# Output projection of a small transformer layer transposed and issued between attention steps, on one core

## The chip, the cores and the metric

The kernel runs on one core of a Trainium2 chip. The metric is the device time of one execution in microseconds (us); smaller is better. All times below are microseconds unless marked ns.

## The reference

`x` is 32 sequences of 112 tokens with 512 features. Two layers follow each other; the first is a cross-attention over a context of 375 tokens. The second, which the change touches, takes the 14 best tokens of each sequence by a router score, 448 in all, and runs a transformer block on them:

```
h = rms_norm(sel) ; q, k, v = h@wq+bq, h@wk+bk, h@wv+bv        # 16 query heads, 8 key heads of 128
att = softmax(causal(q_rot @ k_rot.T / sqrt(128)))             # 448 x 448 per head
x1  = sel + (att @ v).reshape(448, 2048) @ wo                  # output projection
mlp = (silu(rms_norm(x1) @ w_gate) * (rms_norm(x1) @ w_up)) @ w_down
out = sigmoid(score) * (x1 + mlp) + (1 - sigmoid(score)) * x   # scattered back to the tokens
```

## The kernel before, in words

The first layer is a software pipeline over 32 sequences and fills most of the span; the change leaves it alone. The second layer works on S = 448 tokens as NC = 4 tiles of L = 112, features as KC = 4 tiles of P = 128. Each engine has its instructions written out in order in its own function, and semaphores tie the engines together. An engine that waits holds up everything behind it on that engine.

Precision: `mm3` (L1211) multiplies two float32 matrices as three products of rounded parts (hi x hi, hi x lo, lo x hi, type fp32r). ScalarE makes the rounded part, GpSimd or VectorE the rest. Attention itself and the output projection use plain float32 matmuls, which the profile shows as two instructions each.

Attention runs over k = 0 to 63, head k // 4, query tile c = k % 4, with (c + 1) x 112 keys. For step k TensorE's `att` (L1471) makes the scores in PSUM bank c and adds the mask (L1472). VectorE takes the negated row maximum (L1146). ScalarE takes the exponential with the row sum (L847), VectorE divides by the sum (L1137, L1140). LAG = 3 steps later TensorE transposes the probabilities (`turn_probs`, L1480) into bank 4 or 5 in turn, and ScalarE empties that bank (`turn_evac`, L837). Once a head's four tiles are there, `weigh` (L1490) multiplies by the values into bank 6 or 7 in turn, and VectorE copies the result to `attnT` (L1152). ScalarE's order in one step is the exponential of k, then emptying of k - 3.

After the last head TensorE makes the projection (L1506) in 128 instructions, with tokens on partitions, one PSUM bank per token tile. VectorE adds the residual (L1170), sums squares (L1173); ScalarE takes the root (L799); VectorE scales (L1097); TensorE transposes 16 tiles (L1439), and the rounded part and the rest (L806, L1111) go to `hT_hi`, `hT_lo`. Meanwhile VectorE computes the sigmoid gates (L1156 to L1167).

The feed-forward loop runs over j = 0 to 15 blocks of 128 hidden features: gate and up products (24 matmuls of 448 columns), SiLU on ScalarE (L879) and VectorE (L1191 to L1197), rounding of the hidden block (L862) and its rest (L1184), and two blocks later `down`, 12 matmuls of 512 columns with tokens on partitions. GpSimd makes the rests of the weights (L620, L629). At the end VectorE adds (L1205) and gates (L1207) each token tile and GpSimd scatters it (L633).

SyncE's queue loads `wo` before attention, w_gate and w_up when attention begins and w_down (4 MB, L455) after the projection, because `w_down` lies where `wo` lay.

## Time and profile before

| | |
|---|---|
| median of 3 runs | 1685.36 us (1683.93 to 1686.45) |
| profiled execution: time / span of its instructions | 1689.02 / 1687.3 us |
| TensorE busy, whole span | 1602.7 us, 95% |
| VectorE / ScalarE / GpSimd busy | 65% / 41% / 40% |
| mean granted TensorE clock | 0.977 |

Rows of the timeline give start (us from the span's start), length, engine, line, operation, output<-inputs, shape and count, and in brackets the idle time before with what ended it. PE is TensorE, DVE VectorE, ACT ScalarE, POOL GpSimd, PEld TensorE's weight loads. Matmuls overlap: the distance between starts, not the length, is what each adds in a full stream. Rows of a stretch give its bounds and length, then busy time and count of PE, PEld, DVE, ACT and POOL, the granted TensorE clock (1.00 is 2.4 GHz, 0.50 is 1.2 GHz), the DMA share and GB/s. Rows of a group end with busy us, mean ns | idle time before.

### The profile page before, as it was taken

Reading aid. Unit: us, or ns where it says so; the run is one execution under the profiler, and the core shown is the slowest. Engines: PE = TensorE matmul, PEld = TensorE weight load, DVE = VectorE, ACT = ScalarE, POOL = GpSimd, SP = SyncE. Lnnn points to the kernel's source line nnn. Section 1 sums busy time; section 2 is a strip of 40 time slices with the busy share of each in tenths; the row PEclk is TensorE's granted clock in tenths of the full one; section 3 lists DMA queues with packets and bytes.
Section 4 is the critical chain, followed back from the end, with each engine's and each line's share of the span. In section 5 each row is a group of like instructions: output and inputs, shape, how many; then the busy total and the mean of one; then the engine's idle time right before and its main releaser. Section 6 shows DMA issues by size and latency. Waiting matters only on the chain.

```text
span 1687.3 us, 43831 instructions
## 1 busy us (share of the span) xinstructions
PE 1602.7 (95%) x17669; PEld 1224.4 (73%) x17669; DVE 1096.7 (65%) x1751; ACT 686.4 (41%) x1406; POOL 678.3 (40%) x758
## 2 busy tenths in 40 slices
PE   7999999999999999999999999999974999898997
PEld 5776777777777777777777777777763876645885
DVE  5754667766767667776677767776663856622766
ACT  5763444344443444434444444434432225511331
POOL 6762443443434443444434434344323950011542
PEclk9999999999999999999999999999985999998999
DMA  6841111221112211121111211122056013002000
GB/s 186 246 123 62 48 53 45 63 68 45 51 45 65 66 45 51 45 74 56 51 45 48 77 51 51 45 63 67 28 190 212 1 40 161 1 0 100 1 1 22
DMA packets 66103, 113.71 MB, mean 67 GB/s; under 512 B 21328, under 2 KB 36016, under 8 KB 64512
## 3 DMA queue, kind: packets, MB, share of 16 engines
q1 hardware_dynamic: 65216, 110.20, 20.6%
q0 software_dynamic: 832, 2.75, 0.6%
q8 instruction: 37, 0.61, 0.2%
q14 instruction: 18, 0.15, 0.0%
HBM read 82.59 MB, written 30.34 MB: 67 GB/s over the span
## 4 chain that ended last, share of the span: by engine, by line
PE 91%; DVE 3%; ACT 2%; issue 1%; DMA 1%; POOL 1%; SPq 0%; ACTq 0%; DVEq 0%; POOLq 0%
PE ps L1213 20%; PE ps L1214 17%; PE ps L1215 17%; PE ps L1340 11%; PE ps L1315 7%; PE ps L1506 3%; PE ps L1265 3%; PE ps L1288 3%; PE ps L1490 2%; PE ps L1318 1%; PE ps L1471 1%; PE ps L1480 1%; PE ps L1247 1%; PE ps L1295 1%; PE ps L1228 0%
## 5 line engine op out<-in xcount | busy, mean ns | idle before, releaser
L939 DVE RECIPROCAL rec<-ps 128x224 f32<-128x224 f32 x128 | 199.2, 1556 | 98.6 <-PE ps L1340 95.6
L499 POOL TENSOR_TENSOR prob_img<-prob 128x448 f32<-128x448 f32 x128 | 157.4, 1230 | 235.9 <-PE ps L1340 214.7
L462 POOL TENSOR_TENSOR ctx_lo<-ctx_raw,ctx_hi 128x472 fp32r<-128x472 f32 x64 | 115.3, 1826 | 288.7 <-ACT ctx_hi L644 288.7
L701 ACT ACTIVATE prob<-ps 119x448 f32<-119x448 f32 x128 | 69.7, 545 | 249.3 <-PE ps L1318 249.3
L934 DVE TENSOR_REDUCE top<-ps 112x4 f32<-112x1028 f32 x128 | 156.2, 1221 | 0.0
L1315 PEld LDWEIGHTS ps<-q_all,k_all 32*128 32x128 f32 (+1 forms) x3072 | 121.6, 186 | 40.1 <-issue 31.8
L1315 PE MATMUL ps<-q_all,k_all 32*128 32x112 f32 (+1 forms) x3072 | 148.0, 300 | 1.4 <-ACT prob L703 1.4
L933 DVE TENSOR_REDUCE top<-ps 112x4 f32<-112x472 f32 x128 | 83.0, 648 | 84.7 <-PE ps L1288 84.7
L677 ACT ACTIVATE sq_junk<-proj 128x513 bf16<-128x513 f32 (+1 forms) x96 | 61.1, 637 | 184.4 <-DVE proj L913 184.4
L703 ACT ACTIVATE prob<-ps 128x896 f32<-128x896 f32 x128 | 117.0, 914 | 0.0
L620 POOL TENSOR_TENSOR ring_lo<-ring,gate_up_hi 128x512 fp32r<-128x512 f32 x32 | 42.1, 1338 | 169.8 <-ACT gate_up_hi L855 169.8
L1213 PE MATMUL ps<-w_v_img_hi,ctx_hi 128*128 128x512 f32 x256 | 107.3, 419 | 0.5
L1213 PE MATMUL ps<-w_k_img_hi,ctx_hi 128*128 128x512 f32 x256 | 107.4, 420 | 0.0
L1215 PE MATMUL ps<-w_v_img_hi,ctx_lo 128*128 128x512 f32 x256 | 101.1, 395 | 0.0
L1215 PE MATMUL ps<-w_k_img_hi,ctx_lo 128*128 128x512 f32 x256 | 101.1, 395 | 0.0
L1214 PE MATMUL ps<-w_k_img_lo,ctx_hi 128*128 128x512 f32 x256 | 100.9, 394 | 0.0
L1214 PE MATMUL ps<-w_v_img_lo,ctx_hi 128*128 128x512 f32 x256 | 100.9, 394 | 0.0
L1215 PE MATMUL ps<-hT_hi,ring_lo 128*128 128x448 f32 x224 | 83.6, 373 | 0.0
L1318 PE MATMUL ps<-topT,pick_img 32*128 32x112 f32 x1024 | 80.8, 296 | 0.0
L493 POOL TENSOR_TENSOR rstd<-sq_sum,neg_half 128x1 f32<-128x1 f32 x96 | 52.8, 549 | 56.1 <-ACT sq_junk L677 56.1
L967 DVE SCALAR_TENSOR_TENSOR equal<-ps,score_now,later 112x112 f32<-112x112 f32 x32 | 10.7, 335 | 92.7 <-PE ps L1300 92.7
L1213 PEld LDWEIGHTS ps<-w_v_img_hi,ctx_hi 128*128 128x128 f32 x256 | 47.9, 187 | 21.7 <-DVE proj L913 7.7
(297 smaller groups left out, 4372.5 us busy)
## 6 DMA issues: line engine op xcount, KB each, us to landing
ctx_raw<-in_ctx_dram SPq DMA_DIRECT2D x32, 748.0 KB, 4.2
xh_dram<-xh SPq DMA_DIRECT2D x32, 448.0 KB, 3.1
q_dram<-q_turned SPq DMA_DIRECT2D x28, 256.0 KB, 2.8
q_all<-q_dram SPq DMA_DIRECT2D x32, 224.0 KB, 3.1
xh<-in_x_dram SPq DMA_DIRECT2D x32, 224.0 KB, 2.8
out_dram<-out_sb SPq DMA_DIRECT2D x32, 224.0 KB, 2.3
xa<-in_x_dram SPq DMA_DIRECT2D x21, 256.0 KB, 3.4
ring<-in_wq_dram SPq DMA_DIRECT2D x1, 4096.0 KB, 13.8
```

The source lines that it names most:

```text
L462: nc.gpsimd.tensor_tensor(ctx_lo[:, :, cols], ctx_raw[:, :, cols], ctx_hi[:, :, cols].bitcast(F32), ALU.subtract).then_inc(ctx_lo_done, 1)
L499: nc.gpsimd.tensor_tensor(prob_img[:], prob[:, g % 2, 1, :], prob[:, g % 2, 2, :], ALU.add).then_inc(img_summed, 1)
L703: nc.scalar.activation(prob[:, g % 2, 1:3, :].rearrange("p c (j q) -> p j c q", j=GH), ps[:, 2:6, L:3 * L].rearrange("p j (c q) -> p j c q ...
L933: nc.vector.tensor_reduce(rows[:, :, 2 * g], ps[0:L, 2:6, 0:TXT], AX.X, ALU.max)
L934: nc.vector.tensor_reduce(rows[:, :, 2 * g + 1], ps[0:L, 2:6, TAIL:CTX], AX.X, ALU.max).then_inc(s_done, 1)
L939: nc.vector.reciprocal(rec[:], bank[:, 2:4]).then_inc(norm_step, 1)
L1213: nc.tensor.matmul(o_, a_hi, b_hi, start=start, stop=False)
L1214: nc.tensor.matmul(o_, a_hi, b_lo, start=False, stop=False)
L1215: return nc.tensor.matmul(o_, a_lo, b_hi, start=False, stop=stop)
L1315: nc.tensor.matmul(ps[0:rows, 2 + j, out_cols], k_all[head, g, cols], q_all[head, g, :], start=True, stop=False)
L1318: last = nc.tensor.matmul(ps[0:rows, 2 + j, out_cols], pick[head, g, :], topT[g // 2][head, :], start=False, stop=True)
L1340: last = nc.tensor.matmul(ps[HD * j:HD * (j + 1), bank, slot * L:(slot + 1) * L], left[0:rows, cols], right[0:rows, L * j:L * (j + 1)], st ...
```

## The change

The projection is turned round: its output and everything after it up to the end of the feed-forward loop has features on partitions and 448 token columns. It uses `mm3` on rounded attention output (`attn_hi`, `attn_lo`) and rounded weights (`wo_hi` by ScalarE, `wo_lo` by GpSimd), and is issued one head at a time inside the attention loop (`output_T`). Its sum stays in PSUM banks 0 to 3 through the loop, so attention has two score banks (4, 5), one for transposes (6) and one for weighing (7). The residual enters that sum as 16 float32 matmuls with the identity (head 0). Sums of squares over partitions are matmuls with a column of ones; the root is transposed back to a row. `down` multiplies into the same four banks, whose contents ScalarE has copied to `mid_raw`; at the end 16 transposes turn the result back. ScalarE empties the transposed tile of step k - 3 before it takes the exponential of step k. The gate computations move to the value products before attention and into its first steps; w_down is loaded in four pieces as the heads of `wo` are used up. The diff, cut (moved gate code, buffers and semaphores left out; 12 leading blanks removed):

```diff
-sp.wait_ge(mid_full, NC)
-sp.dma_start(w_down, t["w_down"].rearrange("(c p) n -> p c n", p=P)).then_inc(ring_loaded[2], 16)
+for e in range(4):
+    sp.wait_ge(ring_loaded[2], 16 * e + 16)
+    if e < 3:
+        sp.wait_ge(o_step, 4 * e + 4)
+    else:
+        sp.wait_ge(mid_full, KC)
+    sp.dma_start(w_down[:, 4 * e:4 * e + 4], t["w_down"].rearrange("(c p) n -> p c n", p=P)[:, 4 * e:4 * e + 4]).then_inc(ring_loaded[2], 16)
...
+for h in range(FH):
+    pool.wait_ge(w_hi_done, FH + FKV + 2 + h + 1)
+    nc.gpsimd.tensor_tensor(wo_lo[:, h, :], wo[:, h, :], wo_hi[:, h % 2].bitcast(F32), ALU.subtract).then_inc(w_lo_done, 1)
...
+act.wait_ge(gate_step, NC)
+nc.scalar.activation(gate_e[:], sel_score[:], ACT.Exp, scale=-1.0).then_inc(gate_exp, 1)
+act.wait_ge(val_ready, 2 * NC)
+act.wait_ge(ring_loaded[2], 16)
...
-                         ps[0:L, 4 + k % 2, 0:(c + 1) * L].rearrange("t (b q) -> t b q", b=c + 1), ACT.Copy).then_inc(pT_ready, 1)
...
-for k in range(FH * NC + LAG):
+                         ps[0:L, 6, 0:(c + 1) * L].rearrange("t (b q) -> t b q", b=c + 1), ACT.Copy).then_inc(pT_ready, 1)
+
+def attn_rounded(h):
+    act.wait_ge(attn_full, h + 1)
+    nc.scalar.activation(attn_hi[:, h, :], ps[:, 7, 0:S], ACT.Copy).then_inc(attn_hi_done, 1)
...
+def wo_rounded(h):
+    if h >= 2:
+        act.wait_ge(o_step, h - 1)
+    nc.scalar.activation(wo_hi[:, h % 2], wo[:, h, :], ACT.Copy).then_inc(w_hi_done, 1)
...
+for k in range(FH * NC + LAG + 2):
+    if LAG <= k < FH * NC + LAG:
+        turn_evac(k - LAG)
     if k < FH * NC:
         c = k % NC
         n_keys = (c + 1) * L
         act.wait_ge(top_ready, k + 1)
         if k > LAG:
             act.wait_ge(pT_full, k - LAG)
-        nc.scalar.activation(prob2[:, k % (LAG + 1), 0:n_keys], ps[0:L, c, 0:n_keys], ACT.Exp, bias=neg_top[:, c:c + 1],
+        nc.scalar.activation(prob2[:, k % (LAG + 1), 0:n_keys], ps[0:L, 4 + k % 2, 0:n_keys], ACT.Exp, bias=neg_top[:, c:c + 1],
                              accum_out=prob_sum[:, c:c + 1]).then_inc(prob_ready, 1)
-    if k >= LAG:
-        turn_evac(k - LAG)
...
+    if k == FH * NC:
+        nc.scalar.activation(table_warm[:], rms_eps[0:L], ACT.Sqrt)
+    if k % NC == 2 and 1 <= k // NC <= FH:
+        wo_rounded(k // NC - 1)
+    if k % NC == 0 and k >= 2 * NC:
+        attn_rounded(k // NC - 2)
+    if k == FH * NC + LAG:
+        act.wait_ge(att_full, FH * NC)
+        act.wait_ge(ring_loaded[0], 32)
+        act.wait_ge(ring_loaded[1], 48)
+        gate_up_rounded(0)
+        gate_up_rounded(1)
+
+for kc in range(KC):
+    act.wait_ge(mid_full, kc + 1)
+    nc.scalar.activation(mid_sq[:, kc, :], ps[:, kc, 0:S], ACT.Square).then_inc(mid_squared, 1)
+act.wait_ge(sums_full, 1)
+nc.scalar.activation(rstd[:], ps[0:L, 4:8, 0], ACT.Sqrt, bias=rms_eps[0:L], scale=1.0 / D).then_inc(root_ready, 1)
+nc.scalar.activation(table_warm[:], rms_eps[0:L], ACT.Exp)
+for kc in range(KC):
+    act.wait_ge(mid_scaled, KC + kc + 1)
+    nc.scalar.activation(hT_hi[:, kc, :], mid_normed[:, kc, :], ACT.Copy).then_inc(hT_hi_done, 1)
+for kc in range(KC):
+    nc.scalar.activation(mid_raw[:, kc, :], ps[:, kc, 0:S], ACT.Copy).then_inc(mid_kept, 1)
...
+    if k in (3, 7, 11, 15):
+        e = k // NC
+        nc.vector.scalar_tensor_tensor(keep[:, e], xh_sel[:, e, 1], gate_e[:, e:e + 1], xh_sel[:, e, 0], ALU.mult, ALU.add).then_inc(gate_step, 1)
+    h = k // NC - 2
+    if k % NC == 1 and h >= 0:
+        dve.wait_ge(attn_hi_done, h + 1)
+        if h >= 2:
+            dve.wait_ge(o_step, h - 1)
+        nc.vector.tensor_tensor(attn_lo[:, h % 2], ps[:, 7, 0:S], attn_hi[:, h, :].bitcast(F32), ALU.subtract).then_inc(attn_ready, 1)
+for kc in range(KC):
+    at = FH + FKV + KC + kc
+    dve.wait_ge(mid_squared, kc + 1)
+    nc.vector.tensor_scalar(mid_normed[:, kc, :], ps[:, kc, 0:S], fvec[:, at:at + 1], None, ALU.mult).then_inc(mid_scaled, 1)
+dve.wait_ge(root_ready, 2)
+nc.vector.reciprocal(rstd[:], rstd[:]).then_inc(rstd_ready, 1)
+dve.wait_ge(root_row_full, 1)
+
+def mid_rest(kc):
+    dve.wait_ge(hT_hi_done, KC + kc + 1)
+    nc.vector.tensor_tensor(hT_lo[:, kc, :], mid_normed[:, kc, :], hT_hi[:, kc, :].bitcast(F32), ALU.subtract).then_inc(hT_ready, 1)
+
+for kc in range(KC):
+    dve.wait_ge(mid_scaled, KC + kc)
+    nc.vector.tensor_tensor(mid_normed[:, kc, :], mid_normed[:, kc, :], ps[:, 7, 0:S], ALU.mult).then_inc(mid_scaled, 1)
+    if kc:
+        mid_rest(kc - 1)
+mid_rest(KC - 1)
...
+for kc in range(KC):
+    dve.wait_ge(down_full, kc + 1)
+    nc.vector.tensor_tensor(processed[:, kc, :], ps[:, kc, 0:S], mid_raw[:, kc, :], ALU.add).then_inc(processed_ready, 1)
+dve.wait_ge(gate_step, 2 * NC + 3)
 for c in range(NC):
-    dve.wait_ge(down_full, c + 1)
-    nc.vector.tensor_tensor(x_mid[:, c], ps[0:L, 4 + c, :], x_mid[:, c], ALU.add).then_inc(sum_ready, 1)
-    dve.wait_ge(sum_ready, c + 1)
-    nc.vector.scalar_tensor_tensor(keep[:, c], x_mid[:, c], gate[:, c:c + 1], keep[:, c], ALU.mult, ALU.add).then_inc(final_ready, 1)
+    dve.wait_ge(turned_back, c + 1)
+    nc.vector.scalar_tensor_tensor(keep[:, c], ps[0:L, 4 + c, :], gate[:, c:c + 1], keep[:, c], ALU.mult, ALU.add).then_inc(final_ready, 1)
...
+pe.wait_ge(head_read, FH + FKV)
+pe.wait_ge(rope_ready, 4)
 def att(k):
     h, c = k // NC, k % NC
     if c == 0:
         pe.wait_ge(head_ready, FH + h // 2 + 1)
-    if k >= NC:
-        pe.wait_ge(prob_ready, k - NC + 1)
-    o_ = ps[0:L, c, 0:(c + 1) * L]
+    if k >= 2:
+        pe.wait_ge(prob_ready, k - 1)
+    o_ = ps[0:L, 4 + k % 2, 0:(c + 1) * L]
     nc.tensor.matmul(o_, qT[:, h, c * L:(c + 1) * L], kT[:, h // 2, 0:(c + 1) * L], start=True, stop=False)
     nc.tensor.matmul(o_[:, c * L:(c + 1) * L], ident_bf[:], causal[:], start=False, stop=True).then_inc(att_full, 1)
 
 def turn_probs(k):
     c = k % NC
     pe.wait_ge(prob_scaled, k + 1)
-    if k >= 2:
-        pe.wait_ge(pT_ready, k - 1)
+    if k:
+        pe.wait_ge(pT_ready, k)
+    else:
+        pe.wait_ge(val_ready, 2 * NC)
     for b in range(c + 1):
-        last = nc.tensor.transpose(ps[0:L, 4 + k % 2, b * L:(b + 1) * L], prob2[:, k % (LAG + 1), b * L:(b + 1) * L], ident[0:L, 0:L])
+        last = nc.tensor.transpose(ps[0:L, 6, b * L:(b + 1) * L], prob2[:, k % (LAG + 1), b * L:(b + 1) * L], ident[0:L, 0:L])
     last.then_inc(pT_full, 1)
 
 def weigh(h):
     pe.wait_ge(pT_ready, NC * h + NC)
-    if h == 0:
-        pe.wait_ge(val_ready, 2 * NC)
-    if h >= 2:
-        pe.wait_ge(attn_ready, h - 1)
+    if h:
+        pe.wait_ge(attn_ready, h)
     for b in range(NC):
-        last = nc.tensor.matmul(ps[:, 6 + h % 2, b * L:S], vals[:, b, (h // 2) * FD:(h // 2 + 1) * FD], probT[h % 2][:, b, b * L:S],
+        last = nc.tensor.matmul(ps[:, 7, b * L:S], vals[:, b, (h // 2) * FD:(h // 2 + 1) * FD], probT[h % 2][:, b, b * L:S],
                                 start=b == 0, stop=b == NC - 1)
     last.then_inc(attn_full, 1)
 
+def sum_squares(kc):
+    pe.wait_ge(mid_squared, kc + 1)
+    for c in range(NC):
+        last = nc.tensor.matmul(ps[0:L, 4 + c, 0:1], mid_sq[:, kc, c * L:(c + 1) * L], ones_col[:], start=kc == 0, stop=kc == KC - 1)
+    return last
+
+def output_T(h):
+    pe.wait_ge(attn_ready, h + 1)
+    pe.wait_ge(w_lo_done, FH + FKV + 2 + h + 1)
+    for kc in range(KC):
+        if h == FH - 1 and kc == KC - 1:
+            sum_squares(0)
+        cols = slice(kc * P, (kc + 1) * P)
+        last = mm3(ps[:, kc, 0:S], wo_hi[:, h % 2, cols], wo_lo[:, h, cols], attn_hi[:, h, :], attn_lo[:, h % 2], h == 0, h == FH - 1)
+        if h == 0:
+            for c in range(NC):
+                last = nc.tensor.matmul(ps[:, kc, c * L:(c + 1) * L], xh_sel[:, c, 1, cols], ident[0:L, 0:L], start=False, stop=False)
+        if h == FH - 1:
+            last.then_inc(mid_full, 1)
+    if h < FH - 1:
+        last.then_inc(o_step, 1)
+
 pe.wait_ge(consts2, 2)
-for k in range(FH * NC + LAG + 2):
+for k in range(FH * NC + 2 * LAG + 1):
     if k < FH * NC:
         att(k)
     if LAG <= k < FH * NC + LAG:
         turn_probs(k - LAG)
-    if k > NC + LAG and (k - LAG) % NC == 1:
-        weigh((k - LAG) // NC - 1)
-pe.wait_ge(ring_loaded[2], 16)
-pe.wait_ge(attn_ready, FH)
+    if k % NC == 0 and k >= 2 * NC:
+        weigh(k // NC - 2)
+    if k % NC == 2 and k >= 2 * NC + 2:
+        output_T(k // NC - 2)
+for kc in range(1, KC):
+    last = sum_squares(kc)
+last.then_inc(sums_full, 1)
+pe.wait_ge(rstd_ready, 2)
 for c in range(NC):
-    for h in range(FH):
-        last = nc.tensor.matmul(ps[0:L, c, :], attnT[:, h, c * L:(c + 1) * L], wo[:, h, :], start=h == 0, stop=h == FH - 1)
-    last.then_inc(mid_full, 1)
-turn_tokens(1)
-pe.wait_ge(hT_ready, 2 * KC)
-pe.wait_ge(mid_ready, NC)
+    last = nc.tensor.transpose(ps[:, 7, c * L:(c + 1) * L], rstd[:, c:c + 1].to_broadcast([L, P]), ident[0:L, 0:L])
+last.then_inc(root_row_full, 1)
 
 def down(j):
     pe.wait_ge(m_lo_done, j + 1)
     pe.wait_ge(down_lo_done, j + 1)
-    for c in range(NC):
-        cols = slice(c * L, (c + 1) * L)
-        last = mm3(ps[0:L, 4 + c, :], m_hi[:, j % 2, cols], m_lo[:, j % 2, cols], down_hi[:, j % 3], w_down_lo[:, j, :],
-                   j == 0, j == FC - 1)
+    if j == 0:
+        pe.wait_ge(mid_kept, KC)
+    for kc in range(KC):
+        cols = slice(kc * P, (kc + 1) * P)
+        last = mm3(ps[:, kc, 0:S], down_hi[:, j % 3, cols], w_down_lo[:, j, cols], m_hi[:, j % 2, :], m_lo[:, j % 2, :], j == 0, j == FC - 1)
         if j == FC - 1:
             last.then_inc(down_full, 1)
...
         for e, lo in enumerate((w_gate_lo, w_up_lo)):
             for kc in range(KC):
-                last = mm3(ps[:, 2 * (j % 2) + e, 0:S], gate_up_hi[:, j % 3, e, kc, :], lo[:, kc, j * P:(j + 1) * P],
+                if j == 0 and e == 0:
+                    pe.wait_ge(hT_ready, KC + kc + 1)
+                last = mm3(ps[:, 4 + 2 * (j % 2) + e, 0:S], gate_up_hi[:, j % 3, e, kc, :], lo[:, kc, j * P:(j + 1) * P],
                            hT_hi[:, kc, :], hT_lo[:, kc, :], kc == 0, kc == KC - 1)
         last.then_inc(mlp_full, 1)
     if j >= 2:
         down(j - 2)
+for c in range(NC):
+    for kc in range(KC):
+        if c == 0:
+            pe.wait_ge(processed_ready, kc + 1)
+        last = nc.tensor.transpose(ps[0:L, 4 + c, kc * P:(kc + 1) * P], processed[:, kc, c * L:(c + 1) * L], ident[:])
...
```

## Rows read from the trace of the kernel before

**Rows 1.** Page, chain that ended last: shares of the span by engine.

```profile
PE 91%; DVE 3%; ACT 2%; issue 1%; DMA 1%; POOL 1%; SPq 0%; ACTq 0%; DVEq 0%; POOLq 0%
```

**Rows 2.** Stretches: attention, projection, norm, feed-forward loop, tail.

```profile
1386.10:1481.80 95.70, 84.02 (x482) 59.31 (x480) 63.80 (x210) 55.17 (x193) 0.00 (x0) 1.00 0.22 89
1481.80:1536.99 55.19, 55.16 (x128) 22.54 (x128) 10.93 (x18) 3.57 (x6) 6.44 (x4) 1.00 0.00 1
1536.99:1556.02 19.03, 10.96 (x42) 9.87 (x43) 7.44 (x18) 5.16 (x9) 2.50 (x2) 0.64 0.61 220
1556.02:1666.04 110.02, 109.10 (x517) 94.58 (x516) 77.57 (x74) 36.01 (x70) 52.13 (x41) 1.00 0.00 1
1666.04:1687.30 21.26, 10.10 (x36) 6.89 (x34) 11.25 (x14) 2.11 (x4) 5.10 (x5) 0.83 0.14 43
```

**Rows 3.** Timeline of TensorE, one head of attention.

```profile
1435.20 2.08 PE L1490 MATMUL ps<-over_hT,vals 112*128 112x448 f32 x8
...
1438.46 0.55 PE L1480 MATMUL ps<-ident,rows 112*112 112x112 f32 x4
...
1438.85 0.92 PE L1471 MATMUL ps<-kT,qT 128*112 128x448 f32 x2
...
1439.60 0.21 PE L1472 MATMUL ps<-causal,ident_bf 112*112 112x112 bf16 x1
...
1440.72 0.38 PE L1480 MATMUL ps<-ident,rows 112*112 112x112 f32 x2 [0.55 <-ACT normed L837]
...
1440.93 2.08 PE L1490 MATMUL ps<-normed,vals 112*128 112x448 f32 x8
...
1442.85 0.55 PE L1471 MATMUL ps<-kT,qT 128*112 128x224 f32 x2
```

**Rows 4.** Groups by shape in attention, ScalarE and VectorE.

```profile
L837 ACT ACTIVATE normed<-ps 112x448 f32<-112x448 f32 x8 | 4.3, 534 | 0.0
...
L847 ACT ACTIVATE rows<-ps,neg_top 112x448 f32<-112x448 f32 x16 | 10.2, 635 | 0.6 <-DVE neg_top L1146 0.6
...
L847 ACT ACTIVATE rows<-ps,neg_top 112x112 f32<-112x112 f32 x16 | 5.7, 355 | 0.0
...
L847 ACT ACTIVATION_READ_ACCUMULATOR rows<-ps,neg_top 112x1 f32 x64 | 12.6, 197 | 0.0
...
L1146 DVE TENSOR_REDUCE neg_top<-ps 112x1 f32<-112x448 f32 x16 | 10.0, 624 | 0.2 <-PE ps L1472 0.2
...
L1140 DVE TENSOR_SCALAR rows<-rows,prob_sum 112x448 f32<-112x448 f32 x16 | 7.3, 453 | 0.6
```

**Rows 5.** Stretches: gate/up at first, one gate/up group, one down group.

```profile
1548.30:1554.01 5.71, 5.71 (x16) 5.09 (x16) 0.00 (x0) 0.46 (x1) 1.74 (x2) 0.51 0.33 122
1577.33:1582.17 4.84, 4.84 (x26) 4.49 (x24) 3.27 (x4) 0.00 (x0) 2.86 (x3) 1.00 0.00 0
1582.17:1584.93 2.76, 2.76 (x13) 2.10 (x12) 1.95 (x2) 2.56 (x5) 0.95 (x1) 1.00 0.00 0
```

**Rows 6.** Groups from the norm to the end, VectorE and GpSimd.

```profile
L1184 DVE TENSOR_TENSOR m_lo<-m_prod,m_hi 128x448 fp32r<-128x448 f32 x16 | 11.0, 689 | 0.1
...
L1195 DVE TENSOR_TENSOR rows<-ps,rows 128x448 f32<-128x448 f32 x16 | 10.0, 624 | 0.6
...
L629 POOL TENSOR_TENSOR ring_lo<-ring,down_hi 128x512 fp32r<-128x512 f32 x16 | 20.8, 1302 | 65.5 <-ACT down_hi L886 65.5
```

**Rows 7.** Timeline of the end.

```profile
1677.30 0.69 DVE L1205 TENSOR_TENSOR vals<-ps,vals 112x512 f32<-112x512 f32 x1 [4.72 <-PE ps L1215]
...
1678.88 0.39 PE L1215 MATMUL ps<-down_hi,m_lo 128*112 128x512 f32 x1
...
1682.19 0.75 DVE L1207 SCALAR_TENSOR_TENSOR xh_sel<-vals,gate,xh_sel 112x512 f32<-112x512 f32 x1
...
1683.22 0.94 POOL L633 DMA_INDIRECT out_dram<-xh_sel,tok  x1 [0.45 <-DVE xh_sel L1207]
```

More of the change, by code:

```diff
@@ L597, in _ @@
             pool.wait_ge(rope_ready, 4)
+            nc.gpsimd.memset(ones_col[:], 1.0)
             nc.gpsimd.memset(causal[:], 0.0)
@@ L1161, in _ @@
-            nc.vector.reciprocal(gate[:], gate_e[:]).then_inc(gate_step, 1)
-            dve.wait_ge(gate_step, NC + 2)
-            nc.vector.tensor_scalar(gate_e[:], gate[:], -1.0, 1.0, ALU.mult, ALU.add).then_inc(gate_step, 1)
-            dve.wait_ge(gate_step, NC + 3)
-            for c in range(NC):
-                last = nc.vector.scalar_tensor_tensor(keep[:, c], xh_sel[:, c, 1], gate_e[:, c:c + 1], xh_sel[:, c, 0], ALU.mult, ALU.add)
-            last.then_inc(gate_step, 1)
-            for c in range(NC):
-                dve.wait_ge(mid_full, c + 1)
-                nc.vector.tensor_tensor(x_mid[:, c], ps[0:L, c, :], xh_sel[:, c, 1], ALU.add).then_inc(mid_ready, 1)
```

132 lines of the change are left out of this document (69 added, 63 removed).

## The prediction

> **What bounds the kernel now.** I read the chain of waits first: 91% of the span is TensorE [rows 1]. So the stages come next, cut at the first score product of the feed-forward attention (1386.10), the start and end of the output projection, the first SiLU, the last SiLU and the end [rows 2]. Ahead of 1386.10 the change touches only idle engines, so five stages, 301.2 us, are at stake: attention 95.70, projection 55.19 (TensorE busy throughout), norm with the first gate/up 19.03 (busy 10.96, mean granted clock 0.64), the feed-forward loop 110.02 (busy 109.10), tail 21.26.
>
> The timeline of one head shows what attention is made of. Period: 1440.93 - 1435.20 = 5.73. Inside it 448 score columns take 1438.85 to 1439.60 = 0.75 (so 0.19, 0.38, 0.56 for 112, 224, 336), the mask 0.06 each, four transposes 1438.46 to 1438.85 = 0.39 (ten per head at 0.095), weighing 1440.93 to 1442.85 = 1.92 [rows 3]. Sum 1.88 + 0.24 + 0.95 + 1.92 = 5.0. The other 0.73 is idle, 0.55 of it one wait for ScalarE to empty a transposed tile. TensorE is nearly full already: work moved into attention is not hidden there, it is paid at its own price.
>
> **The change, part by part.** In a full stream, 24 products of 448 columns take 4.84, 0.2017 each, and 12 of 512 columns take 2.76, 0.230 each; at half the clock (1.2 GHz, granted 0.51) 16 of 448 take 5.71, 0.36 each [rows 5].
>
> *Projection.* Removed: 55.19 [rows 2]. Added: 16 heads x 4 tiles x 3 products = 192 x 0.2017 = 38.7. Added with it: the residual as 16 float32 products of 112 columns. They are nearest to the smallest score product, 0.19 [rows 3], so 3.0; at the transposes' price 1.5. Net on TensorE -13.5.
>
> *Attention's idle time.* There are now two score banks, one for transposes, one for weighing. I lay out one head. ScalarE: emptying up to 0.53 for 448 columns; exponential 0.36 to 0.64 plus 0.1 of the 0.20 sum read-out. VectorE: maximum up to 0.62, scaling up to 0.45 [rows 4], smaller sizes in between by their columns. A hand-over costs 0.04 to 0.14 and a matmul's result comes 0.17 after its slot. From the start of a weighing: weigh to 1.92, score to 2.35, three transposes to 2.64, score to 3.26. The next transposes need the single bank emptied (3.25) and start at 3.39 (**wait 0.13**), ending 3.77. The projection needs weighing's result (2.09) rounded by ScalarE (2.72) and its rest taken by VectorE, which has a maximum and a scaling before it: 3.38 to 4.07. So it starts at 4.15 (**wait 0.38**) and ends at 6.57. Score to 7.37, one transpose to 7.47, score to 7.71; the next transposes wait for the bank until 8.04 (**0.33**), and the next weighing starts at 8.23. Work 7.39, idle 0.84, period 8.23. ScalarE gains two roundings (about 0.6 each, as its copies) and stays near 5.2 busy of 8.23; GpSimd, idle here now, gets one subtraction of 1.30 per head [rows 6], a head ahead of its use: both 0. Without that lead the projection would wait 1.9 per head.
>
> *Ends of the stage.* From 1386.10 to the first weighing I keep today's 8.9: a table load in front of the first exponential goes (1.3), and two banks for four and two gate operations on VectorE give it back. Then 14 periods, 115.2; the residual, 3.0; and 12.7 from the 15th weighing to the last projection product (weigh 1.9, wait 1.8, project 2.4, weigh 1.9, round and rest 1.6, project 2.4, column sums 0.7). Sum 139.8 against 95.70 + 55.19 = 150.9: **-11.1**. Bounds: with no idle time 14 x 0.84 less, -23; with a wait of 0.55 at each of four steps, 2.2 per head, +8. I stay at the layout, since its 0.84 is next to today's 0.73.
>
> *Queues.* On SyncE one load of w_down becomes four, each queued behind four projected heads; only the next piece is behind each, and the first is wanted after the norm. 0 now, 0 then. Gate sums move beside the value products, where VectorE has little else: 0.
>
> *Norm.* Now 19.03 from the last projection product to the first SiLU [rows 2]. Then, counted from that product: last square out at 0.76; column sums, 16 two-pass products of one column per pair of tiles, between 0 and 0.095 a pass, the upper price giving 2.45; root, reciprocal and four transposes to 3.7; VectorE multiplies four tiles (0.62) and takes four rests (0.69) [rows 6] to 9.1 while gate/up follows tile by tile; then 3 + 12 products, 3.0 at full clock, 5.4 at half. Today half clock holds for 5.71 from the first gate/up product [rows 5]; I take the same, which makes the first SiLU 13.5: **-5.6** (full clock throughout -6.8, half throughout -4.0).
>
> *Down products.* 448 columns for 512: 12 x 0.028 = 0.34 a group. One group of 16 ends in a wait for VectorE anyway: 15 x 0.34 = **-5.1**. It is 0 only if VectorE became the bound; it is busy 77.57 of 110.02 [rows 2].
>
> *End.* Now the last product's result is at 1679.27 and the fourth scatter starts at 1683.22, 3.95 later, its gatings 1.4 apart [rows 7]. Then: last sum 0.65, transposes 0.75, first gating 0.75 and hand-over 0.3, and four scatters of 0.94 back to back on GpSimd, the fourth at +5.4: **+1.5** (0.7 if VectorE still spaces them).
>
> Sum: -11.1 - 5.6 - 5.1 + 1.5 = -20.3. The profiled execution has span 1687.3 and time 1689.0, so 1668.7 there; it lies 3.7 above the median of the runs shown, and the same difference from that median gives 1685.4 - 20.3 = **1665**.
>
> **A rule against it.** VectorE's subtraction of two SBUF operands takes 0.689 beside the GpSimd stream, its product with a PSUM operand 0.624; one GpSimd subtraction takes 1.30 [rows 6]. The Trainium skill, SBUF — State Buffer, section "SBUF: two separate sides", says that the port pair of the two is an exclusive lock for a whole instruction, against VectorE's 2-port mode or two SBUF inputs. The rows differ by 0.07 and so show little of it. By that rule the time would be the fourth rival's.
>
> **Rivals.**
> 1. *TensorE covers every wait* while the others run ahead during the 2.4 of projection: 14 x 0.84 less, **1653**. For: no other engine is above two thirds of a head. Against: one transposition bank. 10%.
> 2. *Idle near 1.7 per head*, because the rest of the attention tile, behind a maximum and a scaling on VectorE, comes late: +12, **1677**. 10%.
> 3. *Slower: the steps serialise.* Place: score k waits for exponential k-2 and transpose k for emptying k-1. If each score's maximum and exponential end before the next score begins, a head is 7.1 for the four sizes plus 1.92 and 2.42, so 11.5: 14 x 3.3 = +46, **1711**. It decides from a period of 9.7, an idle time of 2.3 per head. Against: I find 0.84. 5%.
> 4. *GpSimd's subtraction stops VectorE's scaling* by up to 1.30 in each of 14 heads: +18, **1683**. Against: in my layout it runs while TensorE projects and VectorE idles. 4%.
> That the change does not do what it says is half of the forecast: "within the attention" hides nothing, idle per head stays near 0.8, and the gain comes from three short passes for float32, the norm and the narrower down products. Emptying before the exponential is worth at most the 0.33 wait.
>
> **How the numbers follow.** Forecast 71%, its own range 1657 to 1674. With rival 1 and all of rival 2, 1652 to 1677. A measurement can tell about 0.2%, 3.4 us, from no change. Slower than that needs rival 3: 0.05; within it is rival 4: 0.04; faster: 0.91.
>
> **What would show it.** Right: 140 from the first score product to the last projection product; weighings 8.2 apart; projection products 0.20 apart; first SiLU 13.5 later; first to last SiLU 105; fourth scatter 5.4 after the last product. Wrong: weighings over 9 apart with a named wait in every head, a scaling that stretches beside GpSimd, or gate/up at half clock well beyond the first tile group.

## The result and the profile after

The changed kernel took **1666.9 us** (median of 4 runs, 1665.8 to 1669.7) where the kernel before took 1685.9 in the runs beside it (4 runs, 1683.9 to 1686.7). The ratio is 0.9892, 95% interval 0.9874 to 0.9909: 19 us faster, against 20 forecast. The profiled execution took 1665.8 with a span of 1664.1. In a later comparison the same kernel gave 1669.2 (5 runs, `after_again`), ratio 0.9890 [0.9875, 0.9905].

Line numbers are from here on those of the changed kernel. TensorE's lines are L1544 score, L1545 mask, L1555 transposes of probabilities, L1563 weighing, L1284 to L1286 the three products of every float32 product, L1583 residual, L1570 column sums. ScalarE's are L903 exponential, L869 emptying, L874 and L886 rounding; GpSimd's L642 is the rest of an output weight. Rows of an experiment carry the line numbers of its own kernel, which lie a few lines off. The chain that ended last still belongs to TensorE, as in [rows 1]:

```profile
PE 92%; DVE 3%; ACT 2%; issue 1%; POOL 1%; DMA 1%; DVEq 0%; ACTq 0%; POOLq 0%; SPq 0%
```

The stretches answer to [rows 2] and have the same columns: start and end, length, busy time and instructions of TensorE, its weight loads, VectorE, ScalarE and GpSimd, then TensorE's granted clock, DMA share, GB/s. Attention and projection are one stretch now, from the first score product to the column sums that follow the last projection product. The others are norm to first SiLU, the loop to the last SiLU, and the tail.

```profile
1382.38:1522.90 140.52, 132.84 (x713) 100.34 (x712) 69.92 (x217) 78.62 (x233) 25.59 (x20) 1.00 0.22 83
1522.90:1535.62 12.72, 10.08 (x54) 9.00 (x53) 5.53 (x11) 7.37 (x14) 1.73 (x2) 0.73 0.26 84
1535.62:1641.49 105.87, 104.88 (x517) 96.82 (x516) 77.76 (x74) 36.11 (x71) 52.95 (x42) 1.00 0.00 1
1641.49:1664.10 22.61, 11.14 (x52) 9.41 (x50) 10.85 (x14) 2.10 (x4) 5.10 (x5) 0.80 0.13 41
```

Against before: 140.5 for 95.7 + 55.2 = 150.9 (-10.4); 12.7 for 19.0 (-6.3); 105.9 for 110.0 (-4.2); 22.6 for 21.3 (+1.4). Together -19.5. The spans of the two profiled executions differ by 23.2; the other 3.7 lie ahead of the first score product (1382.38 for 1386.10), where the change touches idle engines only. In the profiled executions of the experiments that product starts anywhere from 1381.5 to 1384.8, the one with the old code ahead of it (`before_order`) at 1383.9, so most of the 3.7 is variation from one execution to the next.

One head in the new order, TensorE's timeline, answers to [rows 3]:

```profile
1439.06 0.73 PE L1544 MATMUL ps<-kT,qT 128*112 128x336 f32 x2
1439.63 0.21 PE L1545 MATMUL ps<-causal,ident_bf 112*112 112x112 bf16 x1
1439.85 0.57 PE L1555 MATMUL ps<-ident,rows 112*112 112x112 f32 x4
1440.33 0.47 PE L1284 MATMUL ps<-attn_hi,wo_hi 128*128 128x448 f32 x1
1440.64 0.37 PE L1285 MATMUL ps<-attn_lo,wo_hi 128*128 128x448 f32 x1
1440.85 0.37 PE L1286 MATMUL ps<-attn_hi,ring_lo 128*128 128x448 f32 x1
...
1442.88 0.91 PE L1544 MATMUL ps<-kT,qT 128*112 128x448 f32 x2
...
1443.98 0.21 PE L1545 MATMUL ps<-causal,ident_bf 112*112 112x112 bf16 x1
1444.39 0.38 PE L1555 MATMUL ps<-ident,rows 112*112 112x112 f32 x2 [0.20 <-ACT over_hT L869]
1444.61 2.08 PE L1563 MATMUL ps<-normed,vals 112*128 112x448 f32 x8
...
1452.79 0.93 PE L1563 MATMUL ps<-over_hT,vals 112*128 112x448 f32 x2
```

Weighings start 1452.79 - 1444.61 = 8.18 apart. The twelve projection products take 1440.33 to 1442.88 = 2.55 and stand openly in TensorE's stream. Three small gaps are left: about 0.16 before the four transposes (the mask starts at 1439.63 and takes a slot of 0.06), 0.1 before the projection with 0.1 more behind its first product, and 0.36 before the two transposes at 1444.39. The wait for emptying, in the groups by shape over the whole stage, first the kernel before (where emptying is L837), then the changed kernel:

```profile
L1480 PE MATMUL ps<-ident,rows 112*112 112x112 f32 x160 | 26.2, 263 | 10.2 <-ACT normed L837 5.1 <-ACT over_hT L837 3.8 <-DVE rows L1140 1.3
```

```profile
L1555 PE MATMUL ps<-ident,rows 112*112 112x112 f32 x160 | 26.5, 264 | 4.3 <-ACT over_hT L869 2.8 <-ACT normed L869 1.4
```

Idle time ahead of the transposes fell from 10.2 to 4.3, although they now share one bank instead of two. That looked like a detail; the first experiment shows what it is worth.

### The profile page after: what moved, and what is told of

The parts are those of the page before. It is cut to its first block, busy times and chain, and to the rows that moved or that the text cites. A ratio compares the mean times of both kernels' runs of the same rounds, so it can differ in the third digit from the quotient of the medians.

```text
span 1664.1 us, 44189 instructions
## 1 busy us (share of the span) xinstructions
PE 1590.9 (96%) x17801; PEld 1245.3 (75%) x17801; DVE 1092.8 (66%) x1743; ACT 709.6 (43%) x1448; POOL 696.8 (42%) x775
## 4 chain that ended last, share of the span: by engine, by line
PE 92%; DVE 3%; ACT 2%; issue 1%; POOL 1%; DMA 1%; DVEq 0%; ACTq 0%; POOLq 0%; SPq 0%
PE ps L1284 21%; PE ps L1286 18%; PE ps L1285 18%; PE ps L1411 11%; PE ps L1386 7%; PE ps L1336 3%; PE ps L1359 3%; PE ps L1563 2%; PE ps L1544 2%; PE ps L1389 2%; PE ps L1555 1%; PE ps L1318 1%; PE ps L1366 1%; PE ps L1299 1%; ACT q_row L688 0%
## 5 line engine op out<-in xcount | busy, mean ns | idle before, releaser
L1284 PE MATMUL ps<-w_v_img_hi,ctx_hi 128*128 128x512 f32 x256 | 107.6, 420 | 0.6
L1284 PE MATMUL ps<-w_k_img_hi,ctx_hi 128*128 128x512 f32 x256 | 107.5, 420 | 0.0
L1286 PE MATMUL ps<-w_v_img_hi,ctx_lo 128*128 128x512 f32 x256 | 101.3, 396 | 0.0
L1286 PE MATMUL ps<-w_k_img_hi,ctx_lo 128*128 128x512 f32 x256 | 101.1, 395 | 0.0
L1286 PE MATMUL ps<-hT_hi,ring_lo 128*128 128x448 f32 x224 | 83.0, 371 | 0.0
L642 POOL TENSOR_TENSOR ring_lo<-ring,wo_hi 128x512 fp32r<-128x512 f32 x16 | 20.6, 1291 | 128.2 <-ACT wo_hi L886 128.2
L1218 DVE TENSOR_REDUCE neg_top<-ps 112x1 f32<-112x112 f32 (+1 forms) x64 | 28.4, 446 | 57.9 <-PE ps L1545 57.9
```

The costliest lines, as they stand in the source:

```text
L1284: nc.tensor.matmul(o_, a_hi, b_hi, start=start, stop=False)
L1286: return nc.tensor.matmul(o_, a_lo, b_hi, start=False, stop=stop)
```

## The experiments

The theory was my forecast's: the projection's narrower products, the norm and the down products bring the gain, "within the attention" hides nothing, and the order of ScalarE's two steps is worth little. Rivals: the order is the gain; the projection is partly hidden; GpSimd's subtraction costs something on VectorE.

**1. Order undone.** The changed kernel with ScalarE's exponential of tile k ahead of the emptying of tile k-3 again.

```
-                if LAG <= k < FH * NC + LAG:
-                    turn_evac(k - LAG)
                 if k < FH * NC:
...
+                if LAG <= k < FH * NC + LAG:
+                    turn_evac(k - LAG)
```

> The changed kernel with ScalarE's old order: exponential of step k first, then the emptying of step k-3. As predicted (the order is worth at most the 0.33 wait per head): 1667 to 1672. Rival, the hand layout of one head redone with this order: emptying of the one-tile transpose waits for the exponential of 448 columns, so the next transposes start 1.3 later, and those of the four-tile step 0.4 later; period 9.9 for 8.2, in all 24 more: 1691, slower than the kernel before.

Measured: 1691.05 (10 runs, 1688.9 to 1693.0) beside 1686.99, ratio 1.0027 [1.0017, 1.0037]. **Without the new order the rest of the change makes the kernel slower.** The whole loss is in the stage, 163.88 long with TensorE no busier than in the changed kernel, and it is one kind of wait, that of the transposes for ScalarE to empty their bank:

```profile
1383.54:1547.42 163.88, 130.59 (x714) 99.81 (x713) 69.95 (x217) 78.62 (x233) 25.73 (x20) 1.00 0.19 71
```

```profile
L1555 PE MATMUL ps<-ident,rows 112*112 112x112 f32 x160 | 26.6, 264 | 30.6 <-ACT over_hT L869 15.4 <-ACT normed L869 15.1
```

The timelines of TensorE and ScalarE show how it comes about (here L901 is the exponential; the projection's last product starts at 1443.73), first with the order undone, then in the changed kernel:

```profile
1443.93 0.91 PE L1544 MATMUL ps<-kT,qT 128*112 128x448 f32 x2
...
1444.74 0.26 PE L1555 MATMUL ps<-ident,rows 112*112 112x112 f32 x1
...
1445.59 0.63 ACT L901 ACTIVATE rows<-ps,neg_top 112x448 f32<-112x448 f32 x1 [2.63 <-DVE neg_top L1218]
...
1446.22 0.25 ACT L869 ACTIVATE normed<-ps 112x112 f32<-112x112 f32 x1
...
1446.62 0.38 PE L1555 MATMUL ps<-ident,rows 112*112 112x112 f32 x2 [1.37 <-ACT normed L869]
```

```profile
1443.69 0.26 PE L1555 MATMUL ps<-ident,rows 112*112 112x112 f32 x1
...
1443.99 0.26 ACT L869 ACTIVATE over_hT<-ps 112x112 f32<-112x112 f32 x1 [1.94 <-PE ps L1555]
```

ScalarE takes its queue in order. Right behind the score of 448 columns TensorE transposes one tile of an earlier step (1444.74). ScalarE was idle, but it stood at the exponential of that score, which has to wait for VectorE's maximum and then takes 0.63 itself. The emptying of the transposed tile stood behind it and began 1.48 after the transpose, and the next two transposes could only start 1.88 after it. In the changed kernel the two distances are 0.30 and 0.70. So this tile costs 1.2 of each head. The same happens once more at the step before: the four transposes start 1.65 after the three ahead of them (1439.42 to 1441.07), in the changed kernel 1.08 (1438.77 to 1439.85), which is 0.6. About 0.15 comes back, since the projection then follows the four transposes sooner. Weighings are 9.75 apart for 8.18. The length of the projection has no part in it, since in both kernels the score and the transposed tile lie behind the projection. This is the recorded rival, which laid out one head in the old order (1.3 and 0.4 later, period 9.9, 1691); the prediction's 1667 to 1672 did not come.

**2. The order alone, in the kernel before.**

```
             for k in range(FH * NC + LAG):
+                if k >= LAG:
+                    turn_evac(k - LAG)
                 if k < FH * NC:
...
-                if k >= LAG:
-                    turn_evac(k - LAG)
```

> The kernel before with only ScalarE's order changed (emptying first). If the order does what it says with two transposition banks, the one wait of 0.55 (0.7 from issue) per head goes: period 5.73 becomes 5.1, about 10 less, 1676. Rival: another wait takes its place, since the exponential comes 0.3 to 0.5 later: 1684 to 1688.

Measured: 1673.92 (4 runs, 1673.1 to 1676.4), ratio 0.9925 [0.9908, 0.9941]: 13 us from one move. Attention fell from 95.70 to 86.23:

```profile
1383.89:1470.12 86.23, 83.20 (x482) 59.78 (x480) 63.81 (x210) 56.45 (x193) 0.00 (x0) 0.98 0.25 98
```

```profile
1433.69 2.08 PE L1490 MATMUL ps<-normed,vals 112*128 112x448 f32 x8
...
1438.70 2.08 PE L1490 MATMUL ps<-over_hT,vals 112*128 112x448 f32 x8
```

The period is 5.01, which is the 5.0 of work that my sum found in [rows 3]: the whole idle time of 0.73 a head was the emptying behind the exponential. In the kernel before the four transposes of 1438.46 were emptied only from 1440.04 on, behind the exponential of 336 columns that began at 1439.51, and the next transposes into that bank waited for it.

Not all of the 13 is shown to be the order. Fourteen periods are 10.1 shorter and the stage 9.5, since the first weighing came 0.8 later in an execution that had TensorE at 1.2 GHz for a while near the start of the stage (mean clock 0.98). Another 2.2 lie ahead of the stage, where this kernel differs in nothing, and 1.1 in the norm, where 8 gate and up products ran at the half clock and 14 in the kernel before. Both of these vary between executions of one kernel, as experiment 6 shows for the clock.

**3. Is the projection hidden?** Two kernels that leave work out: the first has no projection products for heads 1 to 14, the second leaves out one of the three products of every tile, in all 16 heads.

```
+                if 0 < h < FH - 1:
+                    pe.sem_inc(o_step, 1)
+                    return
```

> The changed kernel without the projection products of heads 1 to 14 (the output lacks them); everything else of them, rounding and rests, stays. If the projection is paid at its own price inside attention, as predicted, the stage from the first score product to the last projection product shortens by 14 x 2.5 = 35. Rival: it also covers waits; by the hand layout the period without it is 6.4, not 5.7, so the stage shortens by 14 x 1.75 = 25.

```
-                    last = mm3(ps[:, kc, 0:S], wo_hi[:, h % 2, cols], wo_lo[:, h, cols], attn_hi[:, h, :], attn_lo[:, h % 2], h == 0, h == FH - 1)
+                    nc.tensor.matmul(ps[:, kc, 0:S], wo_hi[:, h % 2, cols], attn_hi[:, h, :], start=h == 0, stop=False)
+                    last = nc.tensor.matmul(ps[:, kc, 0:S], wo_hi[:, h % 2, cols], attn_lo[:, h % 2], start=False, stop=h == FH - 1)
```

> The changed kernel with two of the three products per projection tile (hi x lo of the weights left out): 4 products of 0.20 fewer per head. If TensorE is the bound at this size of filler, the period falls by all of 0.81, to 7.4, and the stage by 13. If another engine or a chain sets the period, it falls by less than 0.4.

One execution each: 1639.76 and 1655.24. The stage's stretches:

```profile
1384.33:1496.79 112.46, 102.22 (x546) 69.74 (x545) 81.45 (x217) 77.68 (x233) 25.47 (x20) 1.00 0.28 104
```

```profile
1384.66:1512.20 127.54, 119.81 (x649) 88.25 (x648) 69.36 (x217) 78.53 (x233) 25.39 (x20) 1.00 0.25 91
```

A third of the products is worth 140.5 - 127.5 = 13.0, and 64 x 0.2017 is 12.9: at the margin every product is paid in full. All fourteen heads' products are worth 28.1, 2.0 a head of the 2.55 they take. So 0.55 a head is covered. Without the products weighings are 6.14 apart, 5.0 of work and 1.1 idle. The wait for the emptied bank is what it was (4.6 ahead of the transposes over the stage, for 4.3). New are waits of the scores for an exponential to give their bank back: TensorE's weight loads for them wait 4.6 in all, for 2.1. The forecast's "hides nothing" holds at the margin and is off by a fifth over the whole.

**4. Halves.** The projection of a head in two parts, two tiles after the third score of a group and two after the fourth, so that each wait for ScalarE has work in front of it.

```
-                    output_T(k // NC - 2)
+                    h = k // NC - 2
+                    output_T(h, range(2) if h < FH - 1 else range(KC))
+                if k % NC == 3 and k >= 2 * NC + 2:
+                    output_T(k // NC - 2, range(2, KC))
```

> The changed kernel with each projection group in two halves, two tiles after step 4m+2 and two after step 4m+3, so that a filler stands in front of the transposes that wait 0.4 for the emptied bank. If that wait is a matter of order on TensorE, the period falls from 8.18 to 7.8 and the time by 5 to 6, to 1661. Rival: the wait moves to the next transposes and the period stays within 0.1.

Measured: 1663.81 (4 runs, 1660.5 to 1664.9), ratio 0.9869 [0.9851, 0.9886]. The stage is 134.8 long, 5.7 less, and the period 1451.50 - 1443.70 = 7.80, both as expected; the wait is a matter of TensorE's order:

```profile
1443.70 2.08 PE L1563 MATMUL ps<-normed,vals 112*128 112x448 f32 x8
...
1451.50 0.93 PE L1563 MATMUL ps<-over_hT,vals 112*128 112x448 f32 x2
```

The waits before the last transposes and weighing are gone; the one before the four transposes and the first product's 0.1 stay, the latter now twice. The median gives back less of it, 3.1 under the changed kernel's, and the two intervals overlap. In the profiled executions the first score product came 1.4 later than the changed kernel's, and 14 gate and up products ran at the half clock for 8, which makes the norm 0.6 longer; both vary from one execution to the next.

**5. Serial.** Does interleaving pay at all? The attention with its four, two and two banks and emptying first; weighing's raw result kept by a copy on VectorE; then the sixteen heads' projections in a row, in the changed kernel's form with features on partitions. ScalarE's roundings of the first gate and up blocks stand between heads of that row. TensorE's part of the edit:

```
-                if k % NC == 0 and k >= 2 * NC:
-                    weigh(k // NC - 2)
-                if k % NC == 2 and k >= 2 * NC + 2:
-                    output_T(k // NC - 2)
+                if k > NC + LAG and (k - LAG) % NC == 1:
+                    weigh((k - LAG) // NC - 1)
+            for h in range(FH):
+                output_T(h)
```

> The changed kernel with the projection after attention instead of within it: attention with four score banks, two for transposes and two for weighing and ScalarE emptying first, VectorE copying the raw result; then the 16 projection groups of three products back to back. Theory A (issuing within attention costs more than it hides, because it takes banks away): attention 86 as in the run with only the order changed, then 38.7 + 3.2 + 0.7, so 129 from the first score to the last projection product against 140.5, time about 1655. Theory B (interleaving is what the change needs; the run without projection shows 0.55 of 2.55 per head hidden): the tail is not fed by the rounding engines and the stage is 138 or more, time 1664 or more.

Measured: **1657.78** (4 runs, 1656.1 to 1661.3), ratio 0.9843 [0.9826, 0.9859]; its interval lies below the changed kernel's. The stage takes 131.9 for 140.5:

```profile
1382.74:1514.63 131.89, 127.82 (x713) 98.38 (x712) 89.58 (x233) 77.57 (x233) 24.67 (x19) 1.00 0.23 89
```

That is nearer the expected theory A (129, about 1655) than B (138 or more, 1664 or more). That the row of products is not fully fed, as B had it, is part of the 3 beyond 129, and experiments 8 and 9 take it up. Interleaving as the changed kernel does it costs 9. Attention alone with all its banks has a period of 5.01, which with a head's products in a stream (12 x 0.2017 = 2.42) makes 7.43 against 8.18. Only half of that 0.75 can be put down to the banks that the accumulating projection takes: `halves`, with the same banks, has 7.80, so where the products stand in TensorE's order is the other half. That the remaining 0.37 is the banks (two for scores, one each for transposes and weighing) was not tested by a run of its own.

**6. Kept busy.** In the changed kernel five more products into a free bank behind the transposes of the root, which leave everything else alone.

```
+            for _ in range(5):
+                nc.tensor.matmul(ps[:, 6, 0:S], wo_hi[:, 1, 0:P], attn_hi[:, FH - 1, :], start=True, stop=True)
```

> The changed kernel with five more matmuls of 448 columns into an unused bank after the root is turned, while TensorE waits 2.1 for the first gate/up operands. If half clock there comes from the pause alone, some of the 9 half-clock gate/up products run at full clock and the first SiLU comes 0.5 to 1.5 earlier after the last projection product (12.7 now). Rival: no fewer products at half clock, 12.7 to 13.1.

One execution, 1667.93. The first gate products still came at half clock, 0.37 apart:

```profile
1525.02:1527.50 2.48, 2.42 (x25) 2.33 (x23) 0.73 (x2) 0.57 (x2) 0.00 (x0) 1.00 0.37 53
1527.50:1529.50 2.00, 1.50 (x6) 1.45 (x7) 0.63 (x2) 1.73 (x3) 0.00 (x0) 0.50 1.02 396
```

```profile
1528.69 2.21 PE L1607 MATMUL ps<-attn_hi,wo_hi 128*128 128x448 f32 x5
...
1531.60 0.57 PE L1285 MATMUL ps<-hT_lo,gate_up_hi 128*128 128x448 f32 x1
1531.97 0.57 PE L1286 MATMUL ps<-hT_hi,ring_lo 128*128 128x448 f32 x1
```

The first SiLU came 12.7 after the last sums, as without them, so these five buy nothing. But they came too late to say what makes the clock fall. The granted clock was already 0.50 from 1527.50 on, and the five begin at 1528.69. Up to there TensorE was busy with the 24 one-column products of the sums (2.42 of 2.48); the pause that the five fill, 2.07 long in the changed kernel, comes later. So the recorded question, whether that pause brings the half clock, is answered with no: the level is there before it.

How long the half level lasts varies as well. In the profiled execution of the changed kernel 8 gate and up products show the long form (over 0.5), in `after_again`, the same kernel, 16, and the stretch from the last sums to the first SiLU is 14.16 there at a mean clock of 0.64:

```profile
1524.64:1538.80 14.16, 11.52 (x54) 10.23 (x53) 5.53 (x11) 7.37 (x14) 2.52 (x2) 0.64 0.22 76
```

**7. Port.** The changed kernel with the rounding of a head's output weights one step earlier, so that GpSimd's subtraction falls beside VectorE's scaling.

```
-                if k % NC == 2 and 1 <= k // NC <= FH:
+                if k % NC == 1 and 1 <= k // NC <= FH:
```

> The changed kernel with ScalarE's weight rounding one step earlier (4m+1 instead of 4m+2), so that GpSimd's subtraction of 1.29 falls on VectorE's scaling of step 4m+1 (0.34 now) and on its neighbours, where now it falls into VectorE's idle time. By the exclusive port lock a scaling or the subtraction stretches by 0.3 to 1.3. Without one all durations stay within 0.05. In either case the period changes by less than 0.3, since that scaling is not needed before step 4m+4.

One execution, 1668.14. Where the two meet, VectorE's scaling of 224 columns takes 1.37 (1.35 to 1.38 in all 15 places); in the changed kernel, where GpSimd is idle at that point, 0.34:

```profile
1451.15 1.29 POOL L642 TENSOR_TENSOR ring_lo<-ring,wo_hi 128x512 fp32r<-128x512 f32 x1 [6.88 <-ACT wo_hi L886]
1451.21 1.37 DVE L1212 TENSOR_SCALAR rows<-rows,prob_sum 112x224 f32<-112x224 f32 x1
```

```profile
1440.80 0.34 DVE L1212 TENSOR_SCALAR rows<-rows,prob_sum 112x224 f32<-112x224 f32 x1
...
1517.58 2.51 POOL L648 TENSOR_TENSOR ring_lo<-ring,gate_up_hi 128x512 fp32r<-128x512 f32 x2
...
1518.89 0.62 DVE L1229 TENSOR_TENSOR attn_lo<-ps,attn_hi 128x448 fp32r<-128x448 f32 x1 [5.36 <-ACT attn_hi L874]
```

GpSimd's ends at 1452.44 and VectorE's, begun at about the same time, only 0.14 later. The period stayed at 8.18, because TensorE was in the projection meanwhile. The Trainium skill, SBUF — State Buffer, section "SBUF: two separate sides", says that the two share a port pair under an exclusive lock for a whole instruction; these rows agree. The last two rows are the other side of it: a subtraction of VectorE with one operand in PSUM keeps its 0.62 in the middle of two subtractions of GpSimd. The fourth rival's mechanism is real; in the steady heads of the changed kernel the two engines don't meet in that way, and in this run the place where they meet was free of charge.

**8. One engine for both rests.** In `serial` VectorE's rest of the attention tile took 1.35 beside GpSimd's 1.29, ending 0.48 after it, about as if it had only then begun (0.62 alone):

```profile
1475.27 1.29 POOL L645 TENSOR_TENSOR ring_lo<-ring,wo_hi 128x512 fp32r<-128x512 f32 x1 [77.61 <-ACT wo_hi L891]
...
1475.69 1.35 DVE L1241 TENSOR_TENSOR attn_lo<-qT,attn_hi 128x448 fp32r<-128x448 f32 x1 [6.96 <-ACT attn_hi L879]
```

So VectorE takes both from head 2 on, with the changed kernel beside it as a yardstick (`after_again`, whose result stands in the section on the result).

```
-            for h in range(FH):
+            for h in range(2):
                 pool.wait_ge(w_hi_done, FH + FKV + 2 + h + 1)
...
+                if h >= 2:
+                    dve.wait_ge(w_hi_done, FH + FKV + 2 + h + 1)
+                    nc.vector.tensor_tensor(wo_lo[:, h, :], wo[:, h, :], wo_hi[:, h % 2].bitcast(F32), ALU.subtract).then_inc(attn_lo_done, 1)
                 dve.wait_ge(attn_hi_done, h + 1)
```

> The serial kernel with one edit: from head 2 on, the rest of the output weights is taken by VectorE, ahead of the attention's rest, and GpSimd has only its first two. In serial one head of the tail took 2.8, because the two rests overlapped on VectorE and GpSimd and VectorE's grew to 1.35 beside GpSimd's 1.29, so that the inputs of head h+2 were there 2.65 after head h's last product, over the 2.42 that a head's products last. Theory of the shared port: VectorE's two rests in a row last 0.63 + 0.62, the inputs are there 1.95 after, under 2.42, so a head takes 2.42, the last sums start 14 x 0.38 = 5 earlier than in serial (first score to last sums 127 in place of 131.9), in all about 1653, ratio 0.981. Rival, VectorE's 1.35 in serial was not the port but the form of the instruction: it stays 1.35, with the other rest behind it on the same engine the inputs come later than before (2.65 + 0.7), a head takes 3.3 and the kernel is at 1665.

Measured: 1658.9 (5 runs, 1657.3 to 1661.3), ratio 0.9841 [0.9828, 0.9854]: no different from `serial`. The mechanism was right and its sum (1653) wrong twice. VectorE's two rests (L1240 of the weights, L1244 of the attention) took 0.69 and 0.62, and heads followed 2.44 apart:

```profile
1476.47 0.69 DVE L1240 TENSOR_TENSOR ring_lo<-ring,wo_hi 128x512 fp32r<-128x512 f32 x1 [1.24 <-ACT wo_hi L891]
1477.08 0.62 DVE L1244 TENSOR_TENSOR attn_lo<-qT,attn_hi 128x448 fp32r<-128x448 f32 x1
...
1483.79 0.97 DVE L1240 TENSOR_TENSOR ring_lo<-ring,wo_hi 128x512 fp32r<-128x512 f32 x1 [1.21 <-ACT wo_hi L891]
1484.68 1.71 DVE L1244 TENSOR_TENSOR attn_lo<-qT,attn_hi 128x448 fp32r<-128x448 f32 x1
```

But in `serial` the heads had not all taken 2.8, as I wrote from one pair: ScalarE's roundings of weights there start 2.47 and 2.81 apart in turn, so the loss was some 0.37 every second head, 2.6 in all. And the last two rows above are a collision that the sum left out, with GpSimd's rests of the first gate and up blocks, 3.01 for two beside them, where two alone take 2.51; TensorE then waited 0.92, twice. It is not ScalarE's additional rounding there: its rounding of that head's weights began at 1483.13, on time at 2.44 after the last.

**9. Rests apart.** The kernel of experiment 8 with those roundings and rests moved behind the last head.

```
-                if h == 4:
...
-                    gate_up_rounded(0)
-                if h == 7:
-                    gate_up_rounded(1)
                 if h == 10:
                     nc.scalar.activation(table_warm[:], rms_eps[0:L], ACT.Sqrt)
...
+            gate_up_rounded(0)
+            gate_up_rounded(1)
```

> The kernel of serial_one_engine with the rounding of the first two gate and up blocks, and with it GpSimd's rests of them, moved from heads 4 and 7 of the tail to behind its last head. There VectorE's two rests took 0.97 and 1.71 beside GpSimd's 3.01 in place of 0.69 and 0.62, and TensorE waited 0.92 before its first product each time, 1.25 with the wait's own gaps. Theory of the shared port: both waits go, first score to last sums 131.4 - 2 x 1.25 = 128.9, and GpSimd's rests, some 6 from the last head on, end before the norm does (it lasts 5.7 from the last sums to the first gate product), so about 1656, ratio 0.9825. Rival, the port only moves the loss: GpSimd now holds VectorE's products of the norm, the first SiLU comes 2 later after the last sums (15.2 in place of 13.2), and the time stays at 1659.

Measured: **1654.62** (5 runs, 1653.3 to 1657.2), ratio 0.9822 [0.9809, 0.9836]. The stretches are the stage and the norm to the first SiLU:

```profile
1382.92:1511.97 129.05, 125.71 (x713) 99.46 (x712) 87.83 (x247) 77.45 (x233) 5.92 (x5) 1.00 0.23 90
1511.97:1524.90 12.93, 10.29 (x55) 9.13 (x53) 5.53 (x11) 7.38 (x15) 3.95 (x4) 0.74 0.25 82
```

129.05 where 128.9 was expected, and the norm as long as ever. This is the lowest median of the study, 30 us under the kernel before where the change brings 19. Its interval still touches those of `serial` and `serial_one_engine`; what tells it from them is the stage, 129.05 for 131.9 and 131.4.

## Why the prediction was right, and which step was wrong

The time (1665 for 1666.9), its sign and each stage came out, but one step that ranks the parts was wrong.

- **Attention and projection**, -11.1 forecast, -10.4 measured. The hand layout held from point to point, and the ends did too (9.6 to the first weighing for 8.9, 12.9 behind the 15th for 12.7). Counted from the weighing at 1444.61 - 8.18 = 1436.43, the four transposes start at 3.42 (laid out 3.39), the projection at 3.90 (4.15) and ends at 6.45 (6.57), the last transposes start at 7.96 (8.04), the period is 8.18 (8.23). The wait of 0.38 before the projection was about 0.1, with a slower first product instead. The residual took 1396.55 to 1397.36 for one tile, 0.81, so 3.2 for 3.0.
- **The step that failed**: "Emptying before the exponential is worth at most the 0.33 wait". It is worth 23 to 24 us in the new layout (stage 163.9 for 140.5, median 1691.05 for 1666.9) and 9.5 to 13 in the old one. I had put the 0.33 down to the emptying as such and never laid the head out with the old order. There the emptying stands behind the exponential of the newest score, so the wait lasts until that score's maximum and its exponential are through (1.2 a head at the 448-column score, 0.6 at the step before), not for the length of an emptying. The trace of before had the sign of it: the wait of 0.55 for L837 in each head is most of the 0.73 of idle [rows 3].
- It follows that the forecast's account of the gain, "three short passes for float32, the norm, and the narrower down products", is incomplete. The order alone brings the kernel before to 1673.9. With the features on partitions and the projection behind the attention it reaches 1657.8. The move into the attention, as it is placed, gives 9 of that back.
- **"Hides nothing"**: true at the margin (`two_products`), 0.55 of 2.55 a head hidden over the whole (`no_projection`), and more than that lost against a projection behind the attention (0.75 a head in `serial`, half of it by the place in TensorE's order, `halves`).
- **Norm**, -5.6 forecast, -6.3 measured, partly by luck. I took 5.71 at half clock; in this execution it was 3.1 (1528.97 to 1532.10). In `after_again`, with 16 long products, the stretch is 14.16, so -4.9. There the half clock held for 6.11 from the first gate product, near my 5.71, and the stretch is still 0.7 over my 13.5: the steps around it take more than I summed, and the shorter half level hid that.
- **Down products**, -5.1 forecast. The loop is 4.15 shorter, and from the last SiLU to the last product's result 0.67 (12.56 for 13.23): -4.8, 0.34 a group as worked out, for one group fewer.
- **End**, +1.5 forecast, +2.0 measured. The last product's result is at about 1654.05, and the fourth scatter starts at 1660.02, 5.97 later (5.4 forecast). The mis-sized term is the scatters' pace, which I took as 0.94 back to back. The starts are 1.25 apart, with 0.30 between two of them, so three steps last 3.80 for 2.8; what comes ahead of the first was 0.4 shorter than laid out:

```profile
1656.22 0.99 POOL L661 DMA_INDIRECT out_dram<-xh_sel,tok  x1 [11.85 <-DVE xh_sel L1278]
1657.52 0.95 POOL L661 DMA_INDIRECT out_dram<-xh_sel,tok  x1 [0.30 <-DVE xh_sel L1278]
1658.77 0.94 POOL L661 DMA_INDIRECT out_dram<-xh_sel,tok  x1 [0.30 <-issue]
1660.02 0.94 POOL L661 DMA_INDIRECT out_dram<-xh_sel,tok  x1 [0.30 <-issue]
```

- **Rivals.** TensorE did not cover every wait; idle stayed near 0.8, not 1.7. The third one, the steps serialise, came near through one line: with the order undone the kernel is 4 us slower than before and weighings are 9.75 apart, just past the 9.7 from which I had said that rival decides. Only its second half came, transposes that wait for the emptying; the scores did not wait for exponentials (1.4 in the whole stage). I had not seen that the order separated the two.

Left open: what makes the clock fall behind the sums, why the half level lasts for 8 products in one execution and 16 in another of the same kernel, what makes the part ahead of the first score product vary by up to 3 us, and what the four banks cost by themselves.

## What to carry to other kernels

On an engine that takes its queue in order, put the step first whose input is ready first, above all if it frees a bank that another engine wants. An emptying queued behind the exponential of the newest score also waits for that score's maximum and for the exponential itself, here 1.2 us where the emptying takes 0.25. Price such a reordering by laying out one period in both orders: done that way, the order was forecast at 1691 and measured at 1691.

Moving work of the bounding engine between its own waits brings only the waits it covers, here 0.55 of 2.55, and takes banks. Where the moved work stands matters too: cut in two and put ahead of two waits, it gained 5.7 in the stage. Try it behind the loop as well. And look for pairs of SBUF-to-SBUF instructions on VectorE and GpSimd that start within a microsecond of each other: the share of busy time doesn't show that one of them is waiting.
